# A five-stage model in one program: zero fill, row halves, boundary order, early weights, drains and feeds

## The reference: what is computed

```python
h = tok(x)                              # patches @ W + b, normalised, gain, shift
h = h + attn(_layernorm(h), Wq, Wk, Wv, Wo, bo)   # 16 heads of 64, rope, causal softmax
h = h + moe(_layernorm(h), router, w1, w3, w2)    # 4 experts, the top 2 of each token
h = h + rec(_layernorm(h), phazor)      # a complex linear recurrence over the tokens
h = h + ffn(_layernorm(h), gate, up, down)        # 4-bit weights, 16-bit activations
```

## Time and profile before

| | us |
|---|---|
| median of 3 runs | 1939.8 (1936.0 to 1945.2) |
| the profiled execution | 1933.2 |
| its span, first to last instruction | 1931.4 |

### The profile page before, as it was taken

How to read it: one execution, slowest core, us unless ns; L and a number is a source line. 1 busy time by engine, 2 the same in 40 slices (tenths; PEclk the granted TensorE clock), 3 DMA queues, 4 the chain that set the end, 5 groups by cost and what they waited for, 6 DMA issues and landing times. The chain is left out here.

```text
span 1931.4 us, 31390 instructions
## 1 busy us (share of the span) xinstructions
PE 1560.6 (81%) x11301; PEld 1466.0 (76%) x11301; DVE 1269.3 (66%) x2510; ACT 1001.1 (52%) x2154; POOL 1045.7 (54%) x830
## 2 busy tenths in 40 slices
PE   5329898989899989989839999999998836598319
PEld 4228898888888888888839999999997825498219
DVE  6316667666777676666624666666668749657896
ACT  5416565564646474645515554555554424448562
POOL 4336756676766675765526676676765636400000
PEclk8659999999999999989969999999999967799759
DMA  6650000101010100101026555555554331102223
GB/s 218 221 185 1 1 26 1 42 1 42 1 42 1 39 4 2 34 1 34 13 87 194 147 144 139 135 150 136 137 146 118 96 78 32 33 1 107 68 81 113
DMA packets 84146, 147.37 MB, mean 76 GB/s; under 512 B 8056, under 2 KB 61624, under 8 KB 83736
## 3 DMA queue, kind: packets, MB, share of 16 engines
q1 hardware_dynamic: 73480, 131.54, 21.8%
q0 software_dynamic: 10512, 13.83, 4.1%
HBM read 110.34 MB, written 48.37 MB: 82 GB/s over the span
## 5 line engine op out<-in xcount | busy, mean ns | idle before, releaser
L1514 POOL TENSOR_TENSOR expert_w_low<-expert_raw,expert_w_high 128x768 fp32r<-128x768 f32 x152 | 288.8, 1948 | 176.9 <-ACT expert_w_high L1339 171.9
L903 POOL TENSOR_TENSOR qk_low<-rotated,qk_high 128x376 fp32r<-128x376 f32 x128 | 139.4, 1089 | 205.4 <-ACT qk_high L792 204.9
L799 ACT ACTIVATE probs<-psum,neg_max 120x376 f32<-120x376 f32 (+2 forms) x384 | 176.6, 481 | 139.9 <-DVE neg_max L969 122.8
L627 PE MATMUL psum<-diag,probs 128*128 128x128 f32 (+2 forms) x1536 | 211.0, 290 | 31.7 <-DVE pt_low L985 27.3
L627 PEld LDWEIGHTS psum<-diag,probs 128*128 128x128 f32 (+2 forms) x1536 | 191.9, 201 | 39.3 <-ACT raw L786 22.6
L985 DVE TENSOR_TENSOR pt_low<-psum,pt_high 128x752 fp32r<-128x752 f32 x128 | 120.2, 939 | 111.1 <-ACT pt_high L808 110.8
L1486 DVE TENSOR_TENSOR expert_act_low<-expert_act,expert_act_high 128x384 fp32r<-128x384 f32 x152 | 140.2, 923 | 79.6 <-ACT expert_act_high L1377 79.0
L1377 ACT ACTIVATE expert_act_high<-expert_act 128x384 fp32r<-128x384 f32 x152 | 79.8, 525 | 205.2 <-DVE expert_act L1481 205.2
L1298 PE MATMUL psum<-slots_high,expert_w_high 128*128 128x384 f32 x608 | 159.6, 343 | 17.7 <-DVE expert_act L1481 16.4
L808 ACT ACTIVATE pt_high<-psum 128x752 fp32r<-128x752 f32 x128 | 102.7, 802 | 120.0 <-PE psum L627 108.7
L932 POOL TENSOR_TENSOR swapped<-swapped,rope_sin 128x376 f32<-128x376 f32 x128 | 132.5, 1036 | 54.6 <-DVE swapped L962 54.6
(11 more groups left out here) (302 smaller groups left out, 4528.8 us busy)
## 6 DMA issues: line engine op xcount, KB each, us to landing
expert_raw<-in_experts SPq DMA_DIRECT2D x152, 384.0 KB, 3.1
x_slots<-in_c_slots SPq DMA_DIRECT2D x4, 3168.0 KB, 27.3
slot_rows<-x_slots SPq DMA_DIRECT2D x19, 396.0 KB, 4.7
up_spill<-held SPq DMA_DIRECT2D x5, 1128.0 KB, 5.0
held<-up_spill SPq DMA_DIRECT2D x5, 1128.0 KB, 5.6
patch<-in_patches SPq DMA_DIRECT2D x8, 376.0 KB, 6.8
attn_x<-tok_xt SPq DMA_DIRECT2D x8, 376.0 KB, 2.8
attn_x_in<-attn_x SPq DMA_DIRECT2D x8, 376.0 KB
```

The costliest lines, as they stand in the source:

```text
L627: last = pe.matmul(psum[0:nj, BANK_PT + bank, at:at + ni], probs[0:ni, h % 2, src:src + nj], diag[0:ni, h % 2, it, 0:ni], start=True, stop ...
L799: last = act.activation(probs[0:ni, h % 2, at:at + P * it + ni], score_bank(h % 2, it), ACT.Exp, bias=neg_max[0:ni, h % 2, it:it + 1], acc ...
L903: pool.tensor_tensor(qk[1][:, c % 2, k, :], rotated[:, k, :], qk[0][:, c % 2, k, :].bitcast(F32), ALU.subtract).then_inc(qk_ready, 1)
L1514: pool.tensor_tensor(w[1][:, g % RING, :], raw[:, g % RAW, :], w[0][:, g % RING, :].bitcast(F32), ALU.subtract).then_inc(w_low, 1)
```

## The change

1. `tokens_in` stores both halves of the normalised rows: ScalarE's `keep` writes a float32r high half, a new VectorE step `x_low` the low half, one iteration later; `x_dram` has twice the size, and the store moves to iteration i-4. Attention loads the halves into a double buffer; `x_split` and its two tiles are gone, `project` and `values` wait for the load alone. The load for batch b+2 is issued after the batch's residual loads and stores and waits for `proj_made`.
2. The four fills of `x_slots` go behind the seven small loads and the residual rows of batch 0.
3. The scores of pair 0 of the next batch, their maxima, exps and diagonals are made in step 7 (before the first `begin`, for batch 0). `begin` has values of tile 2, output projections, then values of tiles 0 and 1. Residuals and statistics of the batch before follow the low half of tile 2. `weigh`, `place_rows` and `keep_turned` come after the second turned copy of their step. In the last batch 63 of the 72 output matmuls are made in step 7.
4. The four raw weight buffers are allocated before attention and share their place with attention's `raw`, `swapped`, `cos` and `probs`; SyncE loads the first four chunks at attention's end, after `tile_table`.
5. `no_gpsimd_drain=True` on the attention and expert blocks.
6. In the recurrence `keep` and `late_xt` are gone; VectorE multiplies PSUM with `feed` (`feeding`), one batch ahead of the scan. TensorE makes `turn_y` before `turn_x`.

The core of the diff:

```diff
@@ tokens_in
-                for i in range(BATCH + 3):
+                for i in range(BATCH + 4):
...
-                    act.activation(xt[:, u, :, :], psum[:, 4 + 2 * u:6 + 2 * u, 0:TOK], ACT.Copy).then_inc(x_kept, 1)
+                    act.activation(xt[:, u, 0, :, :], psum[:, 4 + 2 * u:6 + 2 * u, 0:TOK], ACT.Copy).then_inc(x_high, 1)
...
+                def x_low(b):
+                    u = b % 2
+                    dve.wait_ge(x_high, b + 1)
+                    dve.tensor_tensor(xt[:, u, 1, :, :], psum[:, 4 + 2 * u:6 + 2 * u, 0:TOK],
+                                      xt[:, u, 0, :, :].bitcast(F32), ALU.subtract).then_inc(x_kept, 1)
...
                         stat(0, i, y[:, i % 2, :, :])
+                    if here(i - 4):
+                        x_low(i - 4)
                     if here(i - 2):
@@ attention
-                for e in range(EXPERTS):
-                    sp.dma_start(x_slots[e * CAPACITY:(e + 1) * CAPACITY, :], a["c_slots"]).then_inc(slots_cleared, 16)
                 sp.dma_start(bo[:], a["token_rows"][:, 3, :]).then_inc(params, 16)
...
-                        sp.wait_ge(attn_x_low, b + 1)
-                        sp.dma_start(xin[:, b % 2, :, :], x_dram[:, :, tokens_of(b + 2)]).then_inc(x_loaded[b % 2], 16)
...
+                    if b == 0:
+                        for e in range(EXPERTS):
+                            sp.dma_start(x_slots[e * CAPACITY:(e + 1) * CAPACITY, :],
+                                         a["c_slots"]).then_inc(slots_cleared, 16)
+                    if b + 2 < BATCH:
+                        sp.wait_ge(proj_made, 2 * PAIRS * (b + 1))
+                        sp.dma_start(x[:, b % 2, :, :, :].bitcast(F32),
+                                     x_dram[:, :, :, tokens_of(b + 2)]).then_inc(x_loaded[b % 2], 16)
+                sp.wait_ge(table_made, 1)
+                e = sp.value_load(where[0:1, 0, 0:1], min_val=0, max_val=EXPERTS - 1)
+                for f in range(RAW_CHUNKS):
+                    sp.dma_start(raw_w[:, f, :], a["experts"][bass.ds(e, 1), f, :, :]
+                                 .rearrange("e p c -> p (e c)")).then_inc(w_in[f], 16)
...
@@ TensorE, step
+                    if c == 0:
+                        pe.wait_ge(v_low, 6 * (b + 1))
                     if c + 1 < PAIRS:
                         scores(b, c + 1)
                     elif more:
-                        pe.wait_ge(exp_made, 16 * b + HEADS + CR_EXP)
-                        values((0, 1))
+                        scores(b + 1, 0)
+                    else:
+                        pe.wait_ge(exp_made, 16 * BATCH + CR_EXP)
+                        pe.wait_ge(o_ready, 8 * b + c + CR_O)
+                        output(b, 0, range(c))
+                        output(b, 1, range(c))
...
@@ TensorE, begin
                     pe.wait_ge(pt_ready, 16 * b + CR_PT)
-                    values((2,))
+                    values(b, (2,))
                     if b:
                         pe.wait_ge(o_ready, 8 * b + CR_O)
                         output(b - 1, 0)
-                    pe.wait_ge(v_low, 6 * b + 4)
-                    scores(b, 0)
-                    if b:
                         pe.wait_ge(raw_made, 16 * b + 2 * LEAD + CR_RAW)
...
                         output(b - 1, 2)
-                    pe.wait_ge(v_low, 6 * b + 6)
+                    pe.wait_ge(exp_made, 16 * b + 2 + CR_EXP)
+                    values(b, (0, 1))
+                    pe.wait_ge(v_low, 6 * b + 2)
@@ VectorE, begin
+                        if b and at == 0:
+                            for k in range(T):
+                                residual(b - 1, k)
+                            stat(b - 1)
                     if b:
-                        residual(b - 1, 0)
-                    maxima(b, 0)
...
+                        inverse(b - 1)
@@ recurrence
+                def feeding(b, k):
+                    u = b % 2
+                    dve.wait_ge(x_turned, b + 1)
+                    dve.tensor_tensor(fed[:, u, k, :, :], psum[:, BANK_X:BANK_X + 2, 0:TOK], feed[:, k, :, :],
+                                      ALU.mult).then_inc((fed_re, fed_im)[k], 1)
...
                         inverse2(i - 2)
+                    if here(i + 1):
+                        for k in range(2):
+                            feeding(i + 1, k)
```

207 lines of the change are left out of this document (89 added, 118 removed).

## The result

| | before | changed kernel | changed kernel, second chip |
|---|---|---|---|
| median, us | 1937.9 (4 runs, 1927.9 to 1945.2) | 1864.4 (4 runs, 1861.8 to 1868.1) | 1858.6 (4 runs; before there: 1939.7) |
| ratio to before | | 0.9625 (0.9578 to 0.9673) | 0.959 (0.9541 to 0.9639) |
| profiled span, us | 1931.4 | 1863.6 | 1858.1 |

Forecast: 1852 us, with 1838 to 1866 as the forecast's own range. The size is nearly right and the parts are not: steady attention gave 13 us (20 in the second profile) of the 35 that I had counted, the end of attention 6 of 10; the way to the first `o_high` and the recurrence gave more than said. To see that, I cut every trace at the same seven events: attention's first load, the first and the last `o_high`, the first expert product, VectorE's memset of `peaks_x` (the recurrence's first instruction), `q_own` (the first of the last stage) and the end.

What follows compares the result with a forecast made beforehand. No engine was taken to bound the whole program; TensorE was busy 36 to 40 of every 40 us in attention and experts. Terms summed to −86.3, from 1933.2 to 1847; with a median allowance, 1852 us (1838 to 1866).

Steps and rivals of the forecast that it cites:

- steady attention: Attention's repeated batches: no split −13, boundary −11, table load −3.5 and clock −8, together −35 us.
- Front: Part ahead of attention: making and storing both row halves, with `x_low` ahead of `stat`, costs +8 us (4 to 11).
- Fill: Attention's start: zero fill behind the small loads brings the first swap earlier, −37 us, with +2 for contention.
- Rivals B and D: Fill: B, fetches or loads starve the prologue, 1865 us, chance 0.11; D, last parameter still lands late, 1867 us, chance 0.03.
- No split: Attention, 7 batches: TensorE's waits for `x_low` and the split's two instructions go, −13 us (−9 to −15).
- The boundary: Between attention's batches: reordered TensorE work removes waits for `pt_low`, −11 us (−14 to +7); moved table load, −3.5.
- The clock: Attention: fewer TensorE waits mean less time at the lower clock level, −8 us (0 to −20).
- Rival A: Attention's boundary gives little, waits change places instead of going: steady attention −12 instead of −35, 1875 us, chance 0.20.
- End of attention: Last batch: 63 of 72 output matmuls move into step 7, −3 us (−7 to 0).
- Early weights: Start of experts: first weights issued while GpSimd scatters bring the first product earlier, −2.8 us (−4 to +1).
- Feeds: Recurrence: feeds on VectorE leave the 11.9 us period unchanged but start earlier, −7 us (−12 to +12).
- rival C: Recurrence: VectorE becomes the bound, feeds held by GpSimd, +10 us instead of −7, 1869 us, chance 0.10.

## Why the prediction was right in size and wrong in its parts

1. *Front*, +8, measured +10.2 (8.5 in the second profile). VectorE's order cost what was said: `x_low` behind `stat` took 3 us off it. What I left out is a wait of ScalarE for the store two batches back, which is now issued one iteration later and twice as large (752 KB, 4.0 us):

```profile
67.01 0.80 ACT L207 ACTIVATE tok_xt<-psum 128x752 fp32r<-128x752 f32 x1 [1.39 <-DMA attn_x<-tok_xt]
...
72.89 0.80 ACT L207 ACTIVATE tok_xt<-psum 128x752 fp32r<-128x752 f32 x1 [0.42 <-DMA attn_x<-tok_xt]
```

2. *Fill*, −37 + 2: the first swap came 11.5 us after the first load instead of 49.2, where I had said 12, and the 2 us for contention were 0: 47.4 us with the fill beside the prologue, 47.5 without. Rivals B and D fall. There was little that the fill could hold up: between its issues and the first `o_high` the trace has two other packets, both instruction fetches: 16 KB in 0.95 us (two took 1.15 and 1.35 without the fill) and 8 KB in 0.38 (0.44 without). The Trainium skill (DMA: Bandwidth & Descriptors, Queues, rings and completion order) says that each engine goes round its queues packet by packet. These two packets do not speak against it; a small load in another queue beside the fill was run in no kernel here.

3. *First scores in the prologue*, −3: from the first swap to the first `o_high` it is 35.9 us instead of 39.8, the missing split of batch 0 included. Together with part 2 the stage was 3.6 us better than said.

4. *No split*, −13: TensorE's wait for `x_low` is gone. The prediction said that the 3.0 us wait in step 5 stays untouched; it fell to 1.9 in the batches with routing. Step 5 went from 17.6 us (mean of batches 0 to 6) to 14.3, 23 us in all, clock included; how much of it is the split was not tested. What the prediction saw in step 5 and put at nothing, GpSimd idle until `qk_high(15)`, was worth 35 us in the kernel before.

5. *The boundary*, −11: this is the step that failed. "`scores(b+1,0)` moves into step 7, so step 7 costs what the others do" counts TensorE's instructions only. It doesn't ask what the moved values had covered: VectorE's `choose`, whose rows I had in the trace. Step 7 and boundary went from 38.5 to 42.9 us in batch 3. The terms of the table load were also mis-sized: −3.5 predicted, about −10 by the run that undid it. I took the 0.5 us wait for the price of a `pt_high` held up, and it was 1.5 in step 2 and 0.4 in step 3. The 1.15 us gap did not move to step 0 and stay, as I had said: TensorE waits 0.4 us there. What the failed step cost is shown by the run with `choose` in pieces, 21 us less in attention than with the block.

6. *The clock*, −8: the granted clock hardly rose, 0.96 and 0.97 in two profiles for 0.96. Low stretches became fewer around step 5, and six of 6.8 us came up in the step 7 of the batches with routing, where none had been. Rival A, waits change places instead of going, is what happened, at 13 to 20 us for the 12 that it named. Its places were wrong: not the outputs and step 0, but `choose`.

7. *End of attention*, −3: the last step grew by 4.0 (4.5 said), and what is behind it shrank by 5.1 up to the last batch's first scatter, net −1. Here too a new wait stands where the old one was: ScalarE may not overwrite the rows before batch 6's scatter has landed, and the rows are now ready earlier than that:

```profile
929.30 1.58 ACT L850 ACTIVATE x_rows<-attn_h,row_shift,row_rstd 128x256 f32<-128x256 f32 x3 [2.75 <-DMA x_slots<-x_rows,slots_u]
```

8. *Drains*, −8.5: right. Put back, they cost 4.3 us at attention's end, and the other row is 4.7 as before.

9. *Early weights*, −2.8: the mechanism was right and its other side missing, the scatter lands 2.3 us later; worth 0.4.

10. *Feeds*, −7, measured −12. The scan pair went to 1.9 us and the start gained 8.4 us up to the fourth batch's first scan (36.3 instead of 44.7 us after the stage's start), as said. Mis-sized was the period: "11.9: no gain in steady state". VectorE is busy 39.59 of 40 us, so it is the bound, at 11.0 us. First the window, then rows of the timeline:

```profile
1555.00:1595.00 40.00, 27.09 (x166) 24.89 (x165) 39.59 (x78) 19.38 (x43) 12.42 (x7) 0.83 0.13 39
```

```profile
1550.57 1.88 DVE L1757 TENSOR_TENSOR_SCAN state<-decay,vectors,fed 128x376 f32<-128x376 f32 x2
...
1558.94 1.78 DVE L1748 TENSOR_TENSOR fed<-psum,recur_feed 128x752 f32<-128x752 f32 x2
...
1561.56 1.88 DVE L1757 TENSOR_TENSOR_SCAN state<-decay,vectors,fed 128x376 f32<-128x376 f32 x2
```

My sum of 11.9 adds durations, and neighbours on VectorE overlap by up to 0.1 us (a row of 1.88 us is followed 1.80 later): the 24 instructions of one iteration add up to 12.5 us and pass in 11.0. A feed took 0.93, as the 0.94 had said, so the held feeds of rival C did not come, though VectorE is the bound. `last_shift` took 1.76, not 1.50.

Summed, the errors are +21.6 in attention's steps, +4.1 at their end and +2.2 in the front, against −3.6 in the prologue, −5.0 in the recurrence and −0.8 elsewhere: 18.5, the difference between −86.3 and −67.8. The times differ by 12 only, because the forecast added 5 us for a median above the profiled execution, and the changed kernel's median is 1 below its own. That the range held is in part luck: without the 9.4 us by which prologue, recurrence and the rest did better than said, the time would have been near 1874.

## What to carry over

When work moves on one engine, list what the other engines do in the place that it leaves, since it may have been their cover; a step's price isn't its own instruction count. A chain of small operations of another engine goes into the free slots between the main chain's operations, what others wait for first, not as a block. And look for the one iteration whose order differs (here the low half of the last projection, once a batch): three lines there took 35 us off the kernel before.

## What the runs showed of the hardware

- Small VectorE operations with two SBUF inputs depend on GpSimd. The compare of 128x48 took 0.20 us at the end of attention, where GpSimd stands, and 1.00 beside it (median of 8: 1.015), so `choose` takes 2.1 us alone and 5.2 in step 7. The Trainium skill (SBUF — State Buffer, Who interferes with whom) says that such an operation contends with a GpSimd instruction that reads SBUF; the trace agrees, with 0.20 against 1.00 us.
- The granted clock fell after a short wait. In the prologue TensorE waited 1.47 us in the changed kernel and 1.99 us in the one with `choose` in step 5, with the same instructions in front, and then

```profile
120.00:122.00 2.00, 2.00 (x10) 1.64 (x9) 1.30 (x4) 1.14 (x2) 1.31 (x2) 1.00 1.04 380
```

```profile
120.00:122.00 2.00, 2.00 (x7) 1.53 (x6) 1.77 (x4) 0.79 (x2) 1.90 (x2) 0.50 0.88 308
```

The second ran at the lower level (1.2 GHz). Its first `o_high` came 1.8 us later, 0.5 of which is the longer wait.
- GpSimd's last scatter, alone, beside two and beside four weight transfers of 384 KB: its last packet ended 2.3, 2.6 and 4.8 us after its issue, and the load that waits for it was issued 4.1, 4.3 and 6.4 us after it.
- Two profiles of the same code differ by 7 us in attention's steps (781.5 and 788.2), since step 6 takes 8.2 to 9.3 and step 7 13.8 to 15.8 us from batch to batch, and chips differ by 1% in the kernel before (1920 and 1940 us): single parts are told apart by stages, not by totals.
